# Normalising attention after the value product instead of before it

## The chip, the cores and the metric

The kernel runs on one core of one Trainium2 chip. The metric is device time in microseconds, from the first to the last instruction of one launch with what lies around it. The core has four compute engines with a queue each: TensorE (PE in the profile: matmuls and transposes, with its weight loads as PEld), VectorE (DVE), ScalarE (ACT) and GpSimd (POOL). A fifth queue, SyncE (SP), issues most of the transfers. The engines wait for each other by semaphores alone.

## The reference

One decoder block over x of 32 sequences of 32 tokens, width 512: cross attention to a context of 257 keys per sequence, then a retention layer, then a feed-forward layer with ternary weights. Only the cross attention is touched here:

```
Q, K, V = split_heads(q @ W_q + b_q), split_heads(k @ W_k + b_k), split_heads(v @ W_v + b_v)   # 16 heads of 32
scores = einsum('bhqd,bhkd->bhqk', Q, K) / sqrt(32); scores = where(mask == 0, -1e9, scores)
attn   = softmax(scores, axis=-1)
out    = einsum('bhqk,bhkd->bhqd', attn, V)          # then @ W_o + b_o, added to x
```

The value bias b_v is added after the value product (variable `bxv`), which is the same since each row of `attn` sums to one.

## The kernel before

The kernel has a start (queries of all 1024 tokens, until about 60 us), a loop over the 32 sequences (the cross attention, until about 510 us), and a tail over 8 tiles of 128 tokens (retention and feed-forward). The program of each engine is written out by hand in its own block, so each queue runs in the order of its code. The loop is software pipelined by one sequence: while the keys and values of sequence b are projected, the softmax and value product of b-1 are done. In the loop:

- **TensorE**, function `sequence` (L419): keys of b in four groups of 12 matmuls (all of them through the helper line L227; each float32 product is three products of float32r parts, high and low), the transpose `turn_mixed` of the result of b-2 (L417), the first half of the values (12 matmuls, L227), `turn` (L395: eight 128x128 transposes of the probabilities of b-1), the second half of the values, `mix` (L409, 64 small matmuls: probabilities times values of b-1), `score` (L386, 32 small matmuls: scores of b). L386 is the last of a sequence, and stands in the trace 32 times for each.
- **VectorE**, function `sequence` (L1086), for sequence b-1: four `mask_scores` (L1044, scaled and masked scores with the row minimum, from a PSUM bank to `probs`); `invert_sums` (L1051) and `normalise` (L1055) for two groups of heads and then for the other two; `keep_output` of b-2 (L1075); `split_context` for b+1 (L999 makes the high part of the context, L1001 the low part); `weigh_last` (L1063: the 257th key's probability times its value, since TensorE handles 256 keys); and `keep_mixed` (L1069: adds that to the value product out of PSUM, to `o_sb`).
- **ScalarE**: exponentials of `probs` with the row sum (L682), copies of keys (L677), values (L687) and of the turned probabilities (L692) out of PSUM. Exponentials 0 and 1 stand ahead of the copy of the first group of keys.
- **GpSimd**: copies the queries of a sequence (`pick_queries`, L870), which waits until the scores of an earlier one are done and so ties GpSimd to TensorE. Between these copies it quantises the feed-forward weights in eight chunks of 128x2048 float32 (`quantise_chunk`, L908, L910, L913: three steps, one chunk in two sequences), about from 190 to 405 us.

`turn` waits for the semaphore `probs_ready`, which L1055 raises; so the transposes stand behind the normalisation. `turn_mixed` waits for `mixed_kept`, which L1069 raises. TensorE starts the keys of b+1 only when `context_split` says that L1001 is done, and puts the fourth group of keys in the bank of the first, once ScalarE has kept that one.

Of the kernel before, what the change touches and what calls it, by code (L numbers as in the profile page):

```python
# [22 lines left out]
ALU = mybir.AluOpType  # L23
# [8 lines left out]
P = 128  # L32
B, S, D = 32, 32, 512
KEYS = 257
KPAD = KEYS + 1
H, DH = 16, 32
C = D // P
# [14 lines left out]
def build_block(nc, x, ctx_t, last_t, mask, ident, decay,  # L52
                w_xq, w_xk, w_xv, w_xo, w_q, w_k, w_v, w_g, w_o, w_1, w_2,
                b_xq, b_xk, b_xv, b_xo, b_g, b_o, gamma, beta, b_1, b_2, last_values, out):
    with ExitStack() as stack:
        def sb(name, shape, dt, offset):
            return nc.alloc_sbuf_tensor_at(name, [P] + shape, dt, offset=BASE + offset)
# [6 lines left out]
        def sem(name):  # L64
            return stack.enter_context(nc.semaphore(name))
# [10 lines left out]
        def vec(name, shape):  # L76

            nonlocal small_at
            t = sb(name, shape, F32, small_at)
            small_at += -(-4 * int(np.prod(shape)) // 32) * 32  # L80
            return t
# [9 lines left out]
        nmax, rowsum, rrow = vec("nmax", [C]), vec("rowsum", [C]), vec("rrow", [C])  # L91
# [31 lines left out]
        last_part, o_sb = sb("last_part", [C, DH], F32, at + 20 * K), sb("o_sb", [C, DH], F32, at + 20 * K + 512)  # L123
# [4 lines left out]
        probs = sb("probs", [C, KEYS], F32, at)  # L128
# [48 lines left out]
        keys_projected, keys_kept = sem("keys_projected"), sem("keys_kept")  # L177
        values_projected, values_kept = sem("values_projected"), sem("values_kept")
        scores_ready, scores_masked, exps_ready = sem("scores_ready"), sem("scores_masked"), sem("exps_ready")
        sums_inverted, probs_ready = sem("sums_inverted"), sem("probs_ready")  # L180
        probs_turned, probs_kept = sem("probs_turned"), sem("probs_kept")
        last_weighed, mixed, mixed_kept = sem("last_weighed"), sem("mixed"), sem("mixed_kept")
        mixed_turned, OT_kept = sem("mixed_turned"), sem("OT_kept")
# [27 lines left out]
        def later(n):  # L211

            return not isinstance(n, int) or n >= 1

        def hold(dve, place, signal, value):

            dve.wait_ge(signal, value)
            dve.memset(carrier[:, place:place + 1], 0.0)
# [101 lines left out]
        def _(pe):  # L320
# [68 lines left out]

            def turn(b):  # L390

                pe.wait_ge(probs_ready, 4 * b + 4)
                for half in range(2):
                    for g in range(C):
                        last = pe.transpose(bank[4 + half][:, g * P:(g + 1) * P],  # L395
                                            probs[:, g, half * P:(half + 1) * P], idf[:, :])
                    last.then_inc(probs_turned, 1)
# [21 lines left out]
            def sequence(b, par):  # L419

                project_keys(b, par)
                if later(b - 1):
                    turn_mixed(b - 2)
                project_values(b, par, 0)
                if later(b):
                    turn(b - 1)
                project_values(b, par, 1)
                score_inputs(b)
                if later(b):
                    mix(b - 1, 1 - par)  # L430
                score(b, par)
# [17 lines left out]
            project_output(0)  # L449
            project_output(1)  # L450
            turn(B - 1)
            project_output(2)
            mix(B - 1, 1)
# [388 lines left out]
        def _(pool):  # L842
# [6 lines left out]
            def invert_deviation(norm, eps, n, n_moments, moments, veps, rstd, t):  # L849

                _, mom, ve, rs = norm
                pool.wait_ge(moments, n_moments)
                pool.tensor_tensor(ve[:, 0:n], mom[:, 0:n, 1], eps[:, 0:n], ALU.add).then_inc(veps, 1)
                pool.wait_ge(veps, t + 1)
                pool.tensor_tensor(rs[:, 0:n], ve[:, 0:n], minus_half[:, 0:n], ALU.pow).then_inc(rstd, 1)
# [108 lines left out]
        def _(dve):  # L964
            def split_weight(n):
                dve.wait_ge(weights_high, n + 1)
                high, low = staged_weights[n][1]
                dve.tensor_tensor(low[:, :, :], stage[n % 2][:, :, :], high[:, :, :].bitcast(F32),
                                  ALU.subtract).then_inc(weights_low, 1)
# [24 lines left out]
            def split_context(b, par):  # L994
                dve.wait_ge(context_landed, 16 * b + 16)
                if later(b - 1):
                    dve.wait_ge(values_projected, 2 * (b - 1))
                high, low = ctxs[par]
                dve.tensor_copy(high[:, :, :], raw[:, :, :]).then_inc(context_high, 1)  # L999
                dve.wait_ge(context_high, b + 1)  # L1000
                dve.tensor_tensor(low[:, :, :], raw[:, :, :], high[:, :, :].bitcast(F32),  # L1001
                                  ALU.subtract).then_inc(context_split, 1)
# [36 lines left out]
            def mask_scores(b, g):  # L1039

                if g == 0 and later(b):
                    hold(dve, 5, last_weighed, b)
                hold(dve, g, scores_ready, 4 * b + g + 1)
                dve.tensor_tensor_reduce(out=probs[:, g, :], in0=bank[4 + g][:, 0:KEYS], in1=mbias[:, :], scale=-SCALE,  # L1044
                                         scalar=BIG, op0=ALU.add, op1=ALU.min,
                                         accum_out=nmax[:, g:g + 1]).then_inc(scores_masked, 1)

            def invert_sums(b, pair_):
                dve.wait_ge(exps_ready, 4 * b + 2 * pair_ + 2)
                part = slice(2 * pair_, 2 * pair_ + 2)  # L1050
                dve.reciprocal(rrow[:, part], rowsum[:, part]).then_inc(sums_inverted, 1)  # L1051

            def normalise(b, g):
                dve.wait_ge(sums_inverted, 2 * b + g // 2 + 1)
                dve.tensor_scalar(probs[:, g, :], probs[:, g, :], rrow[:, g:g + 1], None, ALU.mult).then_inc(probs_ready, 1)  # L1055

            def weigh_last(b, par, nth):

                dve.wait_ge(last_landed[par], 16 * nth + 16)
                if later(b):  # L1060
                    dve.wait_ge(mixed_kept, b)
                hold(dve, 6, probs_ready, 4 * b + 4)
                dve.tensor_tensor(last_part[:, :, :], v_last[par][:, :, :],  # L1063
                                  probs[:, :, KEYS - 1:KEYS].broadcast_to([P, C, DH]), ALU.mult).then_inc(last_weighed, 1)

            def keep_mixed(b):
                dve.wait_ge(last_weighed, b + 1)
                dve.wait_ge(mixed, b + 1)
                dve.tensor_tensor(o_sb[:, :, :], last_part[:, :, :], bank[3][:, 0:P].rearrange("p (g w) -> p g w", g=C),  # L1069
                                  ALU.add).then_inc(mixed_kept, 1)  # L1070

            def keep_output(b):

                dve.wait_ge(mixed_turned, b + 1)
                dve.tensor_tensor(OT[:, :, bass.ds(b * S, S)], bank[3][:, P:2 * P].rearrange("p (j q) -> p j q", j=HG),  # L1075
                                  bxv[:, :].unsqueeze(2).broadcast_to([P, HG, S]), ALU.add).then_inc(OT_kept, 1)

            def softmax(b):
                invert_sums(b, 0)
                normalise(b, 0)  # L1080
                normalise(b, 1)
                invert_sums(b, 1)
                normalise(b, 2)
                normalise(b, 3)

            def sequence(b, par, nth, more=True):  # L1086

                if later(b):
                    for g in range(C):
                        mask_scores(b - 1, g)  # L1090
                if later(b):
                    invert_sums(b - 1, 0)
                    normalise(b - 1, 0)
                    normalise(b - 1, 1)
                if later(b):
                    invert_sums(b - 1, 1)
                    normalise(b - 1, 2)
                    normalise(b - 1, 3)
                if later(b - 1):
                    keep_output(b - 2)  # L1100
                if more:
                    split_context(b + 1, 1 - par)
                else:
                    split_weight(3)
                if later(b):
                    weigh_last(b - 1, 1 - par, nth + par - 1)
                    keep_mixed(b - 1)
# [32 lines left out]
            def output_low(k):  # L1140
                dve.wait_ge(o_high, k + 1)
                part = slice(256 * k, 256 * k + 256)
                dve.tensor_tensor(oT[1][:, :, part], OT[:, :, part], oT[0][:, :, part].bitcast(F32),
                                  ALU.subtract).then_inc(o_low, 1)
# [14 lines left out]
                mask_scores(B - 1, g)  # L1159
            keep_output(B - 2)  # L1160
            output_low(1)
            softmax(B - 1)
            weigh_last(B - 1, 1, B // 2 - 1)
            output_low(2)
            add_output(0)
# [247 lines left out]
```

## Times and profile before

| what | value |
| --- | --- |
| median of 3 runs | 800.01 us (797.69 to 800.78) |
| the profiled execution | 796.09 us |
| its span | 794.1 us |
| TensorE busy | 744.9 us, 94% of the span |
| VectorE busy | 502.2 us, 63% |
| ScalarE busy | 328.4 us, 41% |
| GpSimd busy | 183.1 us, 23% |
| TensorE's mean granted clock | 0.991 |

The profiled execution spends 2.0 us outside its span. A busy time is a sum over the whole program; in the slices of the span one sees TensorE at nine tenths or more from the fourth slice to the last but few, and VectorE much busier in the stretch from about 180 to 410 us than before and after it, though its program is the same there. GpSimd is busy in just that stretch.

### The profile page before, as it was taken

The numbers are of one execution on the slowest core, as the hardware profiler recorded it, in microseconds if no ns is written. First come the engines' busy times: TensorE is split into PE (matmuls) and PEld (weight loads), VectorE is DVE, ScalarE is ACT, GpSimd is POOL, SyncE is SP. The second block draws the span as 40 slices with busy tenths as digits, with TensorE's granted clock in tenths as the row PEclk, the third lists the DMA queues.
The fourth block names the chain that finished last, engine by engine and source line by source line (L and its number), as shares of the span: only waits on it lengthen the run. The fifth ranks groups of instructions, "written<-read, shape, count | busy, mean of one in ns | idle before, by whom it ended". The sixth has DMA issues, their size and how long they took to land.

```text
span 794.1 us, 18836 instructions
## 1 busy us (share of the span) xinstructions
PE 744.9 (94%) x7449; PEld 609.4 (77%) x7464; DVE 502.2 (63%) x1228; ACT 328.4 (41%) x698; POOL 183.1 (23%) x150
## 2 busy tenths in 40 slices
PE   3999999999799999999999999999999999999985
PEld 2778888888687787787788888777777777777742
DVE  6334444345968778778664443485577877877785
ACT  2435464554343343343344444653233343342232
POOL 1500010005945455455420000001101111110010
PEclk9999999999999999999999999999999999999998
DMA  7142333330231231230120112541000000000000
GB/s 258 61 170 78 98 110 131 112 135 30 83 112 35 78 112 34 79 112 30 30 60 31 58 30 93 205 173 54 1 1 14 13 0 13 13 0 14 1 14 26
DMA packets 33956, 53.63 MB, mean 68 GB/s; under 512 B 2416, under 2 KB 23152, under 8 KB 32656
## 3 DMA queue, kind: packets, MB, share of 16 engines
q1 hardware_dynamic: 29168, 36.05, 13.9%
q0 software_dynamic: 3328, 16.78, 5.9%
q10 hardware_dynamic: 1440, 0.53, 0.3%
q8 instruction: 13, 0.21, 0.1%
q14 instruction: 7, 0.06, 0.0%
HBM read 51.19 MB, written 2.16 MB: 67 GB/s over the span
## 4 chain that ended last, share of the span: by engine, by line
PE 80%; issue 8%; DVE 7%; ACT 3%; DMA 1%; DVEq 0%; POOL 0%; SPq 0%; ACTq 0%; POOLq 0%
PE bank L227 56%; PE bank L566 4%; PE bank L395 3%; PE bank L550 3%; PE bank L409 3%; PE bank L515 3%; PE bank L503 2%; PE bank L386 2%; DVE probs L1055 2%; ACT probs L682 1%; DVE ctx_high L999 1%; PE bank L491 1%; PE bank L559 1%; DMA stage<-in_w_xo 1%; DMA X<-in_x 1%
## 5 line engine op out<-in xcount | busy, mean ns | idle before, releaser
L227 PE MATMUL bank<-ctx_high,wk_high 128*128 128x258 f32 x512 | 148.4, 290 | 3.9 <-DVE ctx_low L1001 3.7
L227 PE MATMUL bank<-ctx_low,wk_high 128*128 128x258 f32 x512 | 145.3, 284 | 0.0
L227 PE MATMUL bank<-ctx_high,wk_low 128*128 128x258 f32 x512 | 144.8, 283 | 0.0
L1055 DVE TENSOR_SCALAR probs<-probs,rrow 128x257 f32<-128x257 f32 x128 | 115.7, 946 | 2.3
L227 PEld LDWEIGHTS bank<-ctx_high,wk_high 128*128 128x128 f32 x512 | 97.4, 190 | 17.8 <-issue 17.1
L227 PE MATMUL bank<-wv_high,ctx_high 128*128 128x512 f32 x256 | 106.0, 414 | 0.0
L227 PE MATMUL bank<-wv_low,ctx_high 128*128 128x512 f32 x256 | 101.1, 395 | 0.0
L227 PE MATMUL bank<-wv_high,ctx_low 128*128 128x512 f32 x256 | 100.8, 394 | 0.0
L687 ACT ACTIVATE vals<-bank 128x512 f32<-128x512 f32 x64 | 38.2, 597 | 144.7 <-PE bank L227 144.7
L227 PEld LDWEIGHTS bank<-ctx_low,wk_high 128*128 128x128 f32 x512 | 97.5, 190 | 0.0
L227 PEld LDWEIGHTS bank<-ctx_high,wk_low 128*128 128x128 f32 x512 | 97.2, 190 | 0.0
L1069 DVE TENSOR_TENSOR o_sb<-last_part,bank 128x128 f32<-128x128 f32 x32 | 9.2, 287 | 121.9 <-PE bank L409 121.8
L677 ACT ACTIVATE kT<-bank,bxk 128x257 f32<-128x257 f32 x128 | 60.3, 473 | 59.2 <-PE bank L227 57.2
L682 ACT ACTIVATE probs<-probs,nmax 128x257 f32<-128x257 f32 x128 | 63.8, 501 | 35.1 <-DVE nmax L1044 35.1
L910 POOL TENSOR_SCALAR stage<-stage 128x2048 f32<-128x2048 f32 x8 | 57.1, 7138 | 0.7
L227 PEld LDWEIGHTS bank<-wv_high,ctx_low 128*128 128x128 f32 x256 | 48.1, 188 | 11.4
L1044 DVE CUSTOM_DVE_ANT_0 probs<-bank,mbias 128x257 f32<-128x257 f32 x128 | 47.5, 421 | 11.8 <-issue 11.8
L227 PEld LDWEIGHTS bank<-wv_high,ctx_high 128*128 128x128 f32 x256 | 48.2, 188 | 8.5
L227 PEld LDWEIGHTS bank<-wv_low,ctx_high 128*128 128x128 f32 x256 | 48.3, 188 | 8.4
L870 POOL COPY qs<-qT 128x128 f32<-128x128 f32 (+1 forms) x32 | 9.7, 304 | 184.2 <-PE bank L386 171.1
L395 PE MATMUL bank<-idf,probs 128*128 128x128 f32 x256 | 33.6, 274 | 12.9 <-DVE probs L1055 12.9
L395 PEld LDWEIGHTS bank<-idf,probs 128*128 128x128 f32 x256 | 29.3, 141 | 19.8 <-DVE probs L1055 16.4
(200 smaller groups left out, 1423.3 us busy)
## 6 DMA issues: line engine op xcount, KB each, us to landing
raw<-in_ctx_t SPq DMA_DIRECT2D x32, 514.0 KB, 3.9
stage<-in_w POOLq DMA_DIRECT2D x16, 1024.0 KB, 5.9
X<-in_x SPq DMA_DIRECT2D x4, 512.0 KB, 7.1
v_last<-last_values SPq DMA_DIRECT2D x32, 64.0 KB
out<-X SPq DMA_DIRECT2D x8, 256.0 KB, 2.0
stage<-in_w_xq SPq DMA_DIRECT2D x1, 1024.0 KB, 7.9
stage<-in_w_xk SPq DMA_DIRECT2D x1, 1024.0 KB, 13.1
stage<-in_w_xv SPq DMA_DIRECT2D x1, 1024.0 KB, 5.6
```

The lines of the kernel that those rows point to most:

```text
L227: last = pe.matmul(to, left(i, c), right(j, c), start=(c == 0 and i + j == 0), stop=(c == C - 1 and i == 1))
L395: last = pe.transpose(bank[4 + half][:, g * P:(g + 1) * P], probs[:, g, half * P:(half + 1) * P], idf[:, :])
L409: last = pe.matmul(bank[3][DH * j:DH * (j + 1), g * DH:(g + 1) * DH], pT[:, half, g, j * S:(j + 1) * S], vals[:, par, half, h * DH:(h + 1) ...
L515: last = pe.matmul(bank[7][DH * j:DH * (j + 1), g * P:(g + 1) * P], v_sb[:, h * DH:(h + 1) * DH], s_sb[:, j, g, :], start=True, stop=True)
L550: last = pe.matmul(bank[UP_BANK[n]][:, :], yqT[:, c, :], w1q[:, c, n * 512:(n + 1) * 512], start=(c == 0), stop=(c == C - 1))
L566: last = pe.matmul(bank[to][:, :], hqT[:, f, :], w2q[:, f, :], start=(f == 0), stop=(f == FC - 1))
L677: act.activation(kT[:, m, :], bank[m % 3][:, 0:KEYS], ACT.Identity, bias=bxk[:, m:m + 1]).then_inc(keys_kept, 1)
L682: act.activation(probs[:, g, :], probs[:, g, :], ACT.Exp, bias=nmax[:, g:g + 1], scale=-1.0, accum_out=rowsum[:, g:g + 1]).then_inc(exps_r ...
L687: act.activation(vals[:, par, half, :], bank[1 + half][:, :], ACT.Copy).then_inc(values_kept, 1)
L910: pool.tensor_scalar(at, at, ROUND, 1.0, ALU.subtract, ALU.min).then_inc(ffn_step, 1)
L1044: dve.tensor_tensor_reduce(out=probs[:, g, :], in0=bank[4 + g][:, 0:KEYS], in1=mbias[:, :], scale=-SCALE, scalar=BIG, op0=ALU.add, op1=ALU ...
L1055: dve.tensor_scalar(probs[:, g, :], probs[:, g, :], rrow[:, g:g + 1], None, ALU.mult).then_inc(probs_ready, 1)
```

## The change

The exponentials are no longer divided by their row sums before they are transposed and multiplied with the values. The four row-sum reciprocals become one instruction on 128x4, the four products on 128x257 go, and in `keep_mixed` one product on 128x128 is added: `o_sb` times the reciprocal, each of its four columns spread over the 32 columns of a head. The sum of L1069 then raises a new semaphore (`mixed_summed`), and the product raises `mixed_kept`. `turn` and `weigh_last` wait for the exponentials directly.

```
             def turn(b):
-                pe.wait_ge(probs_ready, 4 * b + 4)
+                pe.wait_ge(exps_ready, 4 * b + 4)
...
-            def invert_sums(b, pair_):
-                dve.wait_ge(exps_ready, 4 * b + 2 * pair_ + 2)
-                part = slice(2 * pair_, 2 * pair_ + 2)
-                dve.reciprocal(rrow[:, part], rowsum[:, part]).then_inc(sums_inverted, 1)
-
-            def normalise(b, g):
-                dve.wait_ge(sums_inverted, 2 * b + g // 2 + 1)
-                dve.tensor_scalar(probs[:, g, :], probs[:, g, :], rrow[:, g:g + 1], None, ALU.mult).then_inc(probs_ready, 1)
+            def invert_sums(b):
+                dve.wait_ge(exps_ready, 4 * b + 4)
+                dve.reciprocal(rrow[:, :], rowsum[:, :]).then_inc(sums_inverted, 1)
...
             def weigh_last(b, par, nth):
-                hold(dve, 6, probs_ready, 4 * b + 4)
+                hold(dve, 6, exps_ready, 4 * b + 4)
...
             def keep_mixed(b):
                 dve.wait_ge(last_weighed, b + 1)
                 dve.wait_ge(mixed, b + 1)
                 dve.tensor_tensor(o_sb[:, :, :], last_part[:, :, :], bank[3][:, 0:P].rearrange("p (g w) -> p g w", g=C),
-                                  ALU.add).then_inc(mixed_kept, 1)
+                                  ALU.add).then_inc(mixed_summed, 1)
+                dve.wait_ge(sums_inverted, b + 1)
+                dve.wait_ge(mixed_summed, b + 1)
+                dve.tensor_tensor(o_sb[:, :, :], o_sb[:, :, :], rrow[:, :].unsqueeze(2).broadcast_to([P, C, DH]),
+                                  ALU.mult).then_inc(mixed_kept, 1)
```

Only VectorE's queue changes its instructions. Its part of one sequence, from the last masked scores on, read before:

```order
L1051 RECIPROCAL rrow<-rowsum 128x2
L1055 TENSOR_SCALAR probs<-probs,rrow 128x257 x2
L1051 RECIPROCAL rrow<-rowsum 128x2
L1055 TENSOR_SCALAR probs<-probs,rrow 128x257 x2
L1075 TENSOR_TENSOR OT<-bank,bxv 128x4x32
L999 CAST ctx_high<-raw 128x1032
L1001 TENSOR_TENSOR ctx_low<-raw,ctx_high 128x1032
L218 MEMSET carrier 128x1
L1063 TENSOR_TENSOR last_part<-v_last_127,probs 128x128
L1069 TENSOR_TENSOR o_sb<-last_part,bank 128x128
```

And it reads now, with the lines of the changed file:

```order
L1050 RECIPROCAL rrow<-rowsum 128x4
L1074 TENSOR_TENSOR OT<-bank,bxv 128x4x32
L999 CAST ctx_high<-raw 128x1032
L1001 TENSOR_TENSOR ctx_low<-raw,ctx_high 128x1032
L218 MEMSET carrier 128x1
L1058 TENSOR_TENSOR last_part<-v_last_127,probs 128x128
L1064 TENSOR_TENSOR o_sb<-last_part,bank 128x128
L1068 TENSOR_TENSOR o_sb<-o_sb,rrow 128x128
```

Five instructions left the place between the masked scores and the sum out of PSUM (the row with x2 stands for two), and L1068 came in as the last one, directly ahead of the masked scores of the next sequence. The other place is VectorE's queue for the last sequence, where the output projection has begun. Before:

```order
L1075 TENSOR_TENSOR OT<-bank,bxv 128x4x32
L1143 TENSOR_TENSOR oT_low<-OT,oT_high 128x4x256
L1051 RECIPROCAL rrow<-rowsum 128x2
L1055 TENSOR_SCALAR probs<-probs,rrow 128x257 x2
L1051 RECIPROCAL rrow<-rowsum 128x2
L1055 TENSOR_SCALAR probs<-probs,rrow 128x257 x2
```

Now:

```order
L1074 TENSOR_TENSOR OT<-bank,bxv 128x4x32
L1128 TENSOR_TENSOR oT_low<-OT,oT_high 128x4x256
L1050 RECIPROCAL rrow<-rowsum 128x4
L218 MEMSET carrier 128x1
L1058 TENSOR_TENSOR last_part<-v_last_127,probs 128x128
L1128 TENSOR_TENSOR oT_low<-OT,oT_high 128x4x256
```

Here the last `turn` no longer stands behind the second `oT_low` (L1143 before, L1128 now) and the four products.

## Rows read from the trace of the kernel before

**Rows 1.** Waits of TensorE, 184 to 413 us: total, times, longest
```profile
PE bank L395 <- DVE probs L1055: 12.6, 7, 1.9
PE bank L227 <- DVE ctx_low L1001: 3.7, 1, 3.7
```
**Rows 2.** The chain of waits in time order: start, length, what
```profile
156.97 5.98 PE bank L227 x48
...
184.69 5.97 PE bank L227 x48
...
193.55 0.87 PE bank L395 x8
...
296.35 6.61 issue
...
303.81 1.09 PE bank L395 x8
...
309.04 5.97 PE bank L227 x48
```
**Rows 3.** Timeline of GpSimd: start, length, what
```profile
192.26 7.43 POOL L910 TENSOR_SCALAR stage<-stage 128x2048 f32<-128x2048 f32 x1
...
200.01 5.38 POOL L913 TENSOR_SCALAR w1q<-stage 128x2048 bf16<-128x2048 f32 x1
...
208.78 7.10 POOL L910 TENSOR_SCALAR stage<-stage 128x2048 f32<-128x2048 f32 x1
...
295.79 7.10 POOL L910 TENSOR_SCALAR stage<-stage 128x2048 f32<-128x2048 f32 x1
309.40 0.29 POOL L870 COPY qs<-qT 128x128 f32<-128x128 f32 x1 [6.52 <-PE bank L386]
309.66 5.37 POOL L913 TENSOR_SCALAR w2q<-stage 128x2048 bf16<-128x2048 f32 x1
```
**Rows 4.** Timeline of VectorE while GpSimd quantises
```profile
192.76 5.43 DVE L1001 TENSOR_TENSOR ctx_low<-raw,ctx_high 128x1032 fp32r<-128x1032 f32 x1
198.12 0.28 DVE L1063 TENSOR_TENSOR last_part<-v_last,probs 128x128 f32<-128x128 f32 x1
...
208.97 7.47 DVE L999 CAST ctx_high<-raw 128x1032 fp32r<-128x1032 f32 x1
...
294.94 8.10 DVE L1055 TENSOR_SCALAR probs<-probs,rrow 128x257 f32<-128x257 f32 x2
```
**Rows 5.** Durations of two lines, ns: minimum, median, maximum
```profile
L1055 DVE TENSOR_SCALAR probs<-probs,rrow x128: 333/354/7265, 61.9 to 517.2; 128x257 f32<-128x257 f32 x128
L1063 DVE TENSOR_TENSOR last_part<-v_last,probs x32: 280/287/3717, 65.8 to 517.8; 128x128 f32<-128x128 f32 x32
```
**Rows 6.** Windows, L386 alone: stretch, length, TensorE busy (count), PEld, clock, DMA
```profile
115.43:143.14 27.71, 1.43 (x64) 0.47 (x64) 1.00 0.37 118
184.69:412.36 227.67, 10.74 (x480) 3.48 (x480) 0.99 0.21 67
184.69:233.60 48.91, 2.15 (x96) 0.70 (x96) 0.97 0.23 79
233.60:398.45 164.85, 7.87 (x352) 2.55 (x352) 1.00 0.20 62
```
**Rows 7.** Windows, all work: PE, PEld, DVE, ACT, POOL busy, clock, DMA
```profile
217.84:221.84 4.00, 4.00 (x20) 4.00 (x21) 3.83 (x3) 0.00 (x0) 4.00 (x1) 0.57 0.00 0
```
**Rows 8.** Timeline of VectorE in an undisturbed sequence
```profile
163.47 0.70 DVE L999 CAST ctx_high<-raw 128x1032 fp32r<-128x1032 f32 x1
164.20 1.23 DVE L1001 TENSOR_TENSOR ctx_low<-raw,ctx_high 128x1032 fp32r<-128x1032 f32 x1
...
170.31 0.29 DVE L1069 TENSOR_TENSOR o_sb<-last_part,bank 128x128 f32<-128x128 f32 x1 [4.66 <-PE bank L409]
```
**Rows 9.** Timeline of ScalarE: the first copy of keys of the sequence from 184.69
```profile
186.38 0.48 ACT L677 ACTIVATE kT<-bank,bxk 128x257 f32<-128x257 f32 x1
```
**Rows 10.** Timeline of TensorE: the last sequence's transposes
```profile
517.64 1.09 PE L395 MATMUL bank<-idf,probs 128*128 128x128 f32 x8 [0.32 <-DVE probs L1055]
```

More of the change, by code:

```diff
@@ L179, in build_block @@
         scores_ready, scores_masked, exps_ready = sem("scores_ready"), sem("scores_masked"), sem("exps_ready")
-        sums_inverted, probs_ready = sem("sums_inverted"), sem("probs_ready")
+        sums_inverted, mixed_summed = sem("sums_inverted"), sem("mixed_summed")
         probs_turned, probs_kept = sem("probs_turned"), sem("probs_kept")
@@ L1076, in keep_output @@
                                   bxv[:, :].unsqueeze(2).broadcast_to([P, HG, S]), ALU.add).then_inc(OT_kept, 1)
[L1078 to L1084, printed above, removed]
             def sequence(b, par, nth, more=True):
@@ L1091, in sequence @@
                 if later(b):
[L1092 to L1098, printed above, removed]
+                    invert_sums(b - 1)
                 if later(b - 1):
@@ L1161, in _ @@
             output_low(1)
-            softmax(B - 1)
+            invert_sums(B - 1)
             weigh_last(B - 1, 1, B // 2 - 1)
```

## The prediction, made before the changed kernel ran

> **What bounds the kernel now.** I read the busy times first. The reader sees TensorE at work for nearly the whole span and VectorE for under two thirds, so time taken off VectorE is worth nothing where TensorE doesn't wait for it. The waits of TensorE tell where it does: between 184 and 413 us it waits seven times for L1055, 12.6 us, and once for L1001, 3.7 us [rows 1]. The chain of waits shows such a place: 6.6 us in which VectorE has a product in hand and waits for nothing that the profile names, and behind them the transposes of TensorE [rows 2]. GpSimd's timeline beside it gives the cause. L910 runs there from 295.79 to 302.89 [rows 3], and the two normalisations that began at 294.94 take 8.10 us, until 303.0 [rows 4]; the line takes 0.354 us in the median and 7.265 at most [rows 5]. This product can't run beside GpSimd's quantisation and stands until that is done.
>
> How much this costs: an undisturbed pair of sequences takes 27.71 us with 64 score matmuls, 32 for each sequence [rows 6], so one sequence takes 13.855. From 184.69 to 412.36 us there are 480 / 32 = 15 sequences in 227.67 us [rows 6]; undisturbed they take 207.83. The quantisation costs 19.8 us. By windows [rows 6]: the 3 sequences up to 233.60 take 48.91 instead of 41.57 (7.3 lost); the next 11 take 164.85 instead of 152.41 (12.4 lost, in six waits, one for each pair); what is left is 0.05. Of the 7.3, 3.7 is the wait for L1001 and some 1.5 the seventh wait for L1055 [rows 1]. In the 4.00 us after the longer one the granted clock is 0.57, between its levels of 1.2 and 2.4 GHz [rows 7], where it is 1.00 in an undisturbed stretch [rows 6]: 4.00 x 0.43 = 1.7 us.
>
> **The change part by part.** *Removed: four products and one reciprocal in each sequence.* Undisturbed they are about 1.4 us of VectorE (4 x 0.354, [rows 5]), worth nothing, since the pair of 27.71 has them. In the disturbed stretch they carry the wait. `turn` comes 193.55 - 184.69 = 8.86 us after the start of a sequence [rows 2]. Two exponentials are done before the first copy of keys at 1.7 (186.38, [rows 9]) and two follow it, so all four are ready before 4, and neither ScalarE nor L1044 (out of PSUM) is held by GpSimd. The six waits go.
>
> *What is late next.* The block doesn't vanish: the next instruction that GpSimd can hold is the cast L999, which took 7.47 us once [rows 4] and takes 0.70 alone [rows 8]. It asks at 163.47 - 156.97 = 6.5 us after a sequence's start [rows 2, 8]. Take the sequence with the L910 at 295.79. It ends at 309.04 [rows 2] and takes 13.86 + 12.4 / 6 = 15.9, so it begins at 293.1. The cast would ask at 299.6, get through at 302.9 with the end of L910 and end at 303.6; L1001 takes 1.23 more [rows 8] and ends at 304.8. TensorE wants it for the next keys at 293.1 + 13.86 = 306.95: 2.1 us are to spare. L1069 waits for the value product until 170.31 - 156.97 = 13.3 anyway [rows 2, 8]. In the other sequence of a pair L913 runs from 0.62 to 6.0 after the start (309.66 for 5.37, start 309.04, [rows 2, 3]) and is over before the cast asks. GpSimd's copy L870 waits for scores [rows 3], so this phase holds in all six pairs. The gain is 12.4, and 0.05 with the last sequence.
>
> *The start of the stretch.* Here GpSimd's steps are not tied to scores. Before, L1055 stood until the L913 from 200.01 was done, and so the cast came behind the second L910 and took until 216.4 [rows 3, 4], L1001 until 217.7. Now the cast of that sequence (start 184.69 + 13.86 = 198.55) asks at 205.0, waits for that L913's end at 205.4, and is done by 206.1, L1001 by 207.4; TensorE wants it at 212.4. The 3.7, the 1.5 and the slow clock go: 7.3. One sequence on, the cast asks at 218.9, the next L913 ends between 221.7 and 222.7 (the second, if VectorE holds GpSimd up by a microsecond at 206), and L1001 is done by 224.6, wanted at 226.3: 1.7 to spare.
>
> *Added: one product on 128x128, L1068.* The nearest row is L1063, the same size with both inputs in SBUF: 0.287 us in the median, 3.717 at most [rows 5]. It stands ahead of the next masked scores, so these, the exponentials and ScalarE's first copy of keys behind two of them move by some 0.3. TensorE needs that copy for its fourth key group, three quarters of 5.97 = 4.5 us after the start [rows 2]; it is done at 186.86 - 184.69 = 2.2 [rows 9]. That leaves 2.3. In the six pairs L1068 runs from 13.65, when GpSimd is still waiting for scores (its copy starts 309.40 - 309.04 = 0.36 after the next start, [rows 2, 3]): free. Only near 212.2 would it meet an L910, the one that starts at 208.78 before [rows 3] and at 208.8 to 209.8 now. L1001 met the L910 of 192.26 and took 5.43, 4.2 longer than alone [rows 4, 8]; but L910's recorded end is 199.69, and L1001 ended at 198.2 and L1063 ran in 0.28 at 198.12 [rows 3, 4]. So a product with two inputs is let through before GpSimd's recorded end, about 4.7 us after L910's start (192.76 + 4.2). L1068 would come through at 213.5 to 214.5, the scores 1.2 to 2.2 us late, inside the 2.3. If it stood until the recorded end (216 to 217), the copy of keys would end near 219, wanted at 216.9: 2 us of TensorE. I take 0, by the row of the same size, with bounds of 0 and 2. Below nothing it can't go, since it takes no work away.
>
> The Trainium skill, "SBUF — State Buffer", section "Who interferes with whom", says that a VectorE instruction with two SBUF inputs contends with a GpSimd instruction that reads SBUF, and that the loser blocks fully, for the whole instruction of the other. By its letter L1068 stands until L910's end, and the sum would be 2 us less. The row of L1063 at 198.12 speaks for an earlier release.
>
> *The last sequence.* `turn` waits 0.32 us for the last product [rows 10], which goes: 0.3. There L1068 falls behind the value product while 12 output matmuls run ahead of the transpose that wants it: 0.
>
> Sum: 12.4 + 0.05 + 7.3 + 0.3 - 0 = 20.1 us. The profiled execution took 796.09 us, 2.0 outside its span of 794.1; it would take 776.0, with a span of 774. The median of the runs shown is 3.9 higher, 800.01, and the same gain gives 779.9, rounded to 780.
>
> **The rivals.** *The start keeps part of its loss.* For: its slacks are small, 1.7 and 0.1 to 1.1, and a wait there costs clock as well [rows 7]. Against: 5 us of slack at the place where it waited before. Price up to 7.3: 787.
>
> *The cast takes the product's place.* For: it is held in every pair, for 3.3 us. Against: 2.1 of slack. Were TensorE to wait for it as it did for L1055, the 12.4 would stay: 792.
>
> *The product was not what `turn` waited for*; the profile names only who came last. Then nothing moves: 800. Against: the end of L910 and the transposes stand together in the rows [rows 2, 3].
>
> *The other side: L1068 is held in every pair.* It has two SBUF inputs and stands ahead of all that a sequence makes of its scores. Were GpSimd to read across the end of a sequence, L1068 would be held 3.4 us (3.717 - 0.287, [rows 5]) to 7.1 (L910, [rows 3]); beyond 2.3 of slack that is 1.1 to 4.8 for each of 15 sequences, 17 to 72 us against 20 gained: 797 to 852. It decides from the point where L870 no longer waits for scores. In the row it waits 6.52 us [rows 3].
>
> **How the numbers follow.** Forecast 0.76; part of the start stays 0.11; cast late 0.05; nothing 0.04; L1068 held 0.04. Half a per cent, 4 us, is about what can be told from no change here. The first three are faster, 0.92; the fourth and the mild end of the fifth are the same, 0.05; slower 0.03. The low end is the forecast for the profiled execution, 776.0, and half a microsecond of scatter: 775.5. The high end takes in the first rival: 787.5.
>
> **What would show it.** Right: TensorE has no wait for VectorE between 184 and 413 us, pairs take 27.7 there as elsewhere, some six or seven casts take 4 us, at most one or two of the two-input products are long, and the clock is 1.00 after 217 us. Wrong: waits of L227 for L1001 in each pair (the cast), of L227 for ScalarE's copy of keys (L1068), or pairs of 29.8 still.

## The result, and the profile after

| | before | after |
| --- | --- | --- |
| median | 799.55 us (4 runs) | 775.5 us (4 runs, 773.9 to 776.97) |
| ratio | 1 | 0.9701 (95%: 0.9668 to 0.9734) |
| in five further rounds | 798.35 us | 776.9 us, 0.9719 (0.9694 to 0.9744) |
| span of the profiled execution | 794.1 us | 772.1 us |
| TensorE's mean granted clock | 0.991 | 0.993 |

The changed kernel is 21 to 24 us faster. I had forecast 780.0, a gain of 20, and a range of 775.5 to 787.5: the time lies on the very edge of the range. The kernel before was profiled in an execution of 796.09 us, the changed one in one of 773.9. One run of the kernel before, beside the five further rounds, took 2244.52 us at a granted clock of 0.33, and no ratio has it in.

In the lines below, L1050 is the reciprocal, L1058 the old L1063, L1064 the old L1069, and L1068 the new product. The waits of TensorE in the last sequence (the answer to [rows 1]; between 183 and 392 us the same view lists none at all):

```profile
PE bank L227 <- DVE oT_low L1128: 1.2, 1, 1.2
...
PE bank L417 <- DVE o_sb L1068: 0.2, 1, 0.2
```

Windows, with the score matmuls alone, as in [rows 6] (stretch, length, TensorE busy and count, PEld, clock, DMA):

```profile
72.42:183.39 110.97, 5.73 (x256) 1.86 (x256) 1.00 0.36 119
183.39:391.65 208.26, 10.74 (x480) 3.49 (x480) 1.00 0.23 73
238.93:377.76 138.83, 7.16 (x320) 2.33 (x320) 1.00 0.23 73
```

The 15 sequences beside GpSimd's quantisation take 208.26 us where they took 227.67: 19.41 us less, and 0.43 more than 15 undisturbed ones. Five pairs take 138.83, so one takes 27.77. The clock, which was 0.57 for 4 us in this stretch [rows 7], is 1.00.

The timeline of VectorE shows where the block went. First at the start of the quantisation, then in a regular pair:

```profile
203.69 0.77 DVE L999 CAST ctx_high<-raw 128x1032 fp32r<-128x1032 f32 x1
204.49 1.23 DVE L1001 TENSOR_TENSOR ctx_low<-raw,ctx_high 128x1032 fp32r<-128x1032 f32 x1
205.65 2.32 DVE L1058 TENSOR_TENSOR last_part<-v_last,probs 128x128 f32<-128x128 f32 x1
...
210.98 1.60 DVE L1068 TENSOR_TENSOR o_sb<-o_sb,rrow 128x128 f32<-128x128 f32 x1
...
217.65 3.60 DVE L999 CAST ctx_high<-raw 128x1032 fp32r<-128x1032 f32 x1
...
259.19 3.88 DVE L999 CAST ctx_high<-raw 128x1032 fp32r<-128x1032 f32 x1
263.11 1.23 DVE L1001 TENSOR_TENSOR ctx_low<-raw,ctx_high 128x1032 fp32r<-128x1032 f32 x1
```

And GpSimd beside it:

```profile
207.92 7.10 POOL L910 TENSOR_SCALAR stage<-stage 128x2048 f32<-128x2048 f32 x1
...
255.43 7.10 POOL L910 TENSOR_SCALAR stage<-stage 128x2048 f32<-128x2048 f32 x1
...
267.02 0.29 POOL L870 COPY qs<-qT 128x128 f32<-128x128 f32 x1 [4.50 <-PE bank L386]
```

These lines show three things. The cast L999 takes 3.88 us in the pair and ends at 263.07, half a microsecond after L910's end at 262.53; L1001 is done at 264.34, while the next keys start at 266.66: 2.3 us to spare. Seven casts take 3.6 us or more, this one and the one at 217.65 among them. L1068 was held only once, at 210.98; it takes 0.29 us in the median. And GpSimd still waits 4.50 us for the scores, which keeps L910 away from L1068.

**Where the 22.0 us between the two spans lie**, from the starts of the same matmuls in both chains of waits and the windows:

| stretch (before; after) | before | after | less |
| --- | --- | --- | --- |
| until the third sequence (73.81; 72.42) | 73.81 | 72.42 | 1.39 |
| 8 undisturbed sequences | 110.88 | 110.97 | -0.09 |
| 15 beside the quantisation | 227.67 | 208.26 | 19.41 |
| 6 undisturbed | 83.14 | 83.17 | -0.03 |
| the last sequence and the output | 29.76 | 28.91 | 0.85 |
| the tail's steady part | 216.65 | 216.65 | 0 |
| the end | 52.19 | 51.72 | 0.47 |

The first 1.39 is no work of the change: the programs are the same there. The chain after the first wait of TensorE, before:

```profile
17.71 5.46 PE bank L227 x12
```

and after:

```profile
17.70 4.42 PE bank L227 x12
```

The same 12 matmuls take 5.46 or 4.42 us, and the 8 transposes behind them 1.25 or 0.87; in both traces the matmuls begin at 0.63 us each and fall to 0.39, after 22.54 in the trace before and after 20.40 in the one after. This 1 us and more is chance: in the second profile of the changed kernel the 12 take 5.03, with the long steps cut (e4) 5.46, and in a kernel with the old softmax (e9) 4.55. It looks like the clock, but the records don't show that: the granted clock from 17 to 23.16 us stands at 1.00 in these profiles. The 0.47 at the end lies where the two windows show clocks of 1.00 and 0.86 before, 0.89 and 0.90 after.

### The profile page after: what moved, and what is told of

Its sections match the earlier page's. It is cut to its first block, busy times and chain, and to the rows that moved or that the text cites. A ratio compares the mean times of both kernels' runs of the same rounds, so it can differ in the third digit from the quotient of the medians.

```text
span 772.1 us, 18699 instructions
## 1 busy us (share of the span) xinstructions
PE 741.4 (96%) x7464; PEld 608.0 (79%) x7464; DVE 408.4 (53%) x1100; ACT 325.5 (42%) x698; POOL 184.0 (24%) x150
## 4 chain that ended last, share of the span: by engine, by line
PE 94%; DVE 4%; ACT 1%; issue 1%; DMA 1%; POOL 0%; DVEq 0%; POOLq 0%
PE bank L227 68%; PE bank L550 4%; PE bank L395 4%; PE bank L566 4%; PE bank L409 3%; PE bank L515 3%; PE bank L386 3%; PE bank L503 2%; PE bank L491 1%; PE bank L559 1%; DMA X<-in_x 1%; PE bank L465 1%; PE bank L522 0%; DVE h_max L1221 0%; PE bank L354 0%
## 5 line engine op out<-in xcount | busy, mean ns | idle before, releaser
L1064 DVE TENSOR_TENSOR o_sb<-last_part,bank 128x128 f32<-128x128 f32 x32 | 9.2, 288 | 123.0 <-PE bank L409 123.0
L910 POOL TENSOR_SCALAR stage<-stage 128x2048 f32<-128x2048 f32 x8 | 57.1, 7138 | 0.7
L1074 DVE TENSOR_TENSOR OT<-bank,bxv 128x128 f32 (+1 forms) x32 | 9.3, 292 | 78.1 <-PE bank L417 78.0
L999 DVE CAST ctx_high<-raw 128x1032 fp32r<-128x1032 f32 x32 | 45.1, 1410 | 1.9 <-DMA raw<-in_ctx_t 1.9
L1001 DVE TENSOR_TENSOR ctx_low<-raw,ctx_high 128x1032 fp32r<-128x1032 f32 x32 | 43.7, 1365 | 1.1
```

What stands on the lines that cost most here:

```text
L910: pool.tensor_scalar(at, at, ROUND, 1.0, ALU.subtract, ALU.min).then_inc(ffn_step, 1)
```

## The experiments

Each ran beside the kernel before on the same chip; times are medians, ratios with 95% intervals.

**The product in another form.** The kernel before, with an added row sum that nobody reads:

```
-                dve.tensor_scalar(probs[:, g, :], probs[:, g, :], rrow[:, g:g + 1], None, ALU.mult).then_inc(probs_ready, 1)
+                dve.tensor_scalar(probs[:, g, :], probs[:, g, :], rrow[:, g:g + 1], 0.0, ALU.mult, ALU.add,
+                                  accum_out=spare_sum[:, g:g + 1]).then_inc(probs_ready, 1)
```

> The kernel before with its four products kept, in their old place and with turn still waiting for them, but each also writes the sum of its row to a spare column. Theory A (the product is held by GpSimd because it takes the second port of SBUF that the two engines share): in this form it takes one port, is never held, costs 0.35 to 0.45 us each time, and TensorE has no wait for L1055 or L1001 between 184 and 413 us. About 19 us of the loop come back as in the changed kernel; only the wait of the last sequence stays: 776 to 779 us. Rival B (VectorE has too much work ahead of the transposes, whatever its form): the work is the same or a little more, so 799 to 801 us. Rival C (any instruction of VectorE that reads and writes SBUF is held): products of 7 us stay, 799 to 801 us.

777.74 us, ratio 0.9733 (0.9693 to 0.9772). The products (minimum, median, maximum in ns) and the cast in its trace:

```profile
L1056 DVE TENSOR_SCALAR_CACHE_REDUCE probs<-probs,rrow x128: 474/480/484, 61.1 to 497.4; 128x257 f32<-128x257 f32 x128
...
L1000 DVE CAST ctx_high<-raw x32: 686/700/3954, 42.9 to 467.9; 128x1032 fp32r<-128x1032 f32 x32
```

A slower product (0.48 instead of 0.354, [rows 5]) that is never held gives back all but 1 to 2 us of what the change gave, with the whole softmax in its old place and more work on VectorE. The cast takes the block, as in the changed kernel. Rivals B and C fall. This is a rule of the Trainium skill too ("SBUF — State Buffer", "Who interferes with whom": the form that also writes out its accumulator stays out of the two-port modes), and the trace agrees, 0.484 at most against 7.265.

**The products back in their place, but not in front of the transposes.** The changed kernel with, in `invert_sums`,

```
+                dve.wait_ge(sums_inverted, b + 1)
+                for g in range(C):
+                    if later(b) or g >= 2:
+                        dve.wait_ge(spared, 4 * b + g - 1)
+                    dve.tensor_scalar(spare[g % 2][:, :], probs[:, g, :], rrow[:, g:g + 1], None, ALU.mult).then_inc(spared, 1)
```

> The changed kernel with four products of the old form in the old place, whose results go to a spare tile that nobody reads, so turn does not wait for them. They are held by GpSimd as before. If the gate in front of the transposes was the cost (theory A): the six waits of a pair go (12.4 us) with the seventh (1.5) and the last (0.3), but at the start of the quantisation the cast again falls behind the second long step of GpSimd, and the wait of 3.7 us for L1001 with the slow clock behind it (1.7) stays: 783 to 787 us. If the work on VectorE is the cost (rival B): all stays, 798 to 801 us. If neither the held product nor its place matter any more once turn is free: 775 to 777 us.

778.7 us, ratio 0.9754 (0.9713 to 0.9794): 3.2 us over the changed kernel's 775.5, 4 us and more under what I expected. Its only new wait in the loop, among TensorE's waits:

```profile
PE bank L229 <- DVE ctx_low L1003: 2.6, 1, 2.6
```

So the direction is right: with the gate gone, the six pairs lose nothing by held products (the products, L1057 here, have a mean of 0.79 us, and a pair takes 27.70), and what stays is the wait for the context at the start, where the pair from 183.94 to 214.48 took 30.54. I had put that wait at 3.7 with 1.7 of clock, as before. Here the cast stood 2.63 us and the instruction behind it, L1003, 5.42, together less than the 8.7 before [rows 4, 8]; the wait was 2.6, and the granted clock in the 4 us after it 1.00.

**GpSimd's steps cut.** Both kernels with `at, to = at[:, 0:16], to[:, 0:16]` ahead of L908, and the rest of the quantised weights set to zero.

> The kernel before with GpSimd's three quantising steps done on 16 of 2048 columns of a chunk (the rest of the quantised weights is zero), so that GpSimd holds nothing for long. Theory A: every sequence takes 13.86 us, products stay at 0.35 us, and 19.8 us go: 776 to 780 us. Rival B: VectorE's work is what it was, 799 to 801 us.

> The changed kernel with the same cut of GpSimd's steps. Theory A: there is nothing left for GpSimd to cost, since its holds of the cast are hidden: 774 to 776.5 us, within 1 us of the changed kernel and 0.3 to 1 us under e3. If holds still cost the changed kernel something: up to 3 us less than 775.5.

Before with the cut: 776.94 us, 0.9723 (0.9683 to 0.9763). After with the cut: 775.55 us, 0.9709 (0.967 to 0.9749). Without GpSimd's long steps the kernel before is 23 us faster, and the changed one no faster than these runs can tell (775.55 and 775.5). The two cut kernels differ by 1.4, with intervals that overlap: without GpSimd's long steps the change by itself is worth that much at most, and perhaps nothing.

**The rival on the other side, made on purpose.** The changed kernel, in which a chunk waits longer before L908:

```
                 pick_queries(2 * n - 6, 0, half)
+                pool.wait_ge(probs_turned, 2 * (2 * n - 8) + 2)
                 quantise_chunk(n, lambda: pick_queries(2 * n - 5, 1, half))
```

> The changed kernel, in which each quantised chunk of GpSimd waits until the transposes of a sequence are done, 9.9 us after the sequence's start, so that its long step L910 lies over the end of the sequence, where L1068 stands. This is the mechanism of the rival on the other side, made on purpose, in six pairs. Theory A (a product with two inputs in SBUF is let through some 4.7 us after L910's start, before its recorded end): L910 runs from 12.0 after the start, L1068 is done at 17.0, the masked scores start 3.1 us late, the first copy of keys ends at 5.2 after the next start and TensorE wants it at 4.5: 0.7 to 1 us for each pair, 4 to 6 in all, 779 to 782 us, with a wait of TensorE for ScalarE's copy of keys. Rule B (held until L910's end at 19.1): 5.2 us late, 3 us for each pair, 18 in all and some slow clock: 793 to 800 us. C (L1068 isn't held by GpSimd): 775 to 776 us.

The second waits for `values_projected, 2 * (2 * n - 7) + 1` instead:

> The same with the chunk waiting for the first half of the values, 8.9 us after the start, so that L910 runs from 11.0 to 18.1. Theory A: L1068 is held from 13.7 until 16.0, the masked scores start 2.1 us late, the first copy of keys ends at 4.2 and is wanted at 4.5: 775 to 777 us, though L1068 takes 2.3 us or more in six pairs. Rule B (held until 18.1): 2 us for each pair, 12 in all: 787 to 790 us. C: as A in time, but L1068 at 0.29 us everywhere.

The third for `probs_kept, 2 * (2 * n - 8) + 2`:

> The changed kernel with each quantised chunk of GpSimd waiting until ScalarE has kept the turned probabilities, 10.5 us after a sequence's start. In the trace of e5 the long step L910 started 11.85 after the start, L1068 was done 4.66 after that, and pairs of sequences took 28.05 instead of 27.75: the slack was just used up. Here L910 starts at 12.55 and L1068 is done at 17.2, 0.7 later. Theory A (release 4.66 after L910's start; each tenth beyond the slack is a tenth of TensorE): pairs of 28.6 to 28.8, six of them, 5 to 6 us above the changed kernel: 780 to 783 us, with TensorE waiting for ScalarE's first copy of keys in the chain. Rule B (release at L910's end): 2.4 more for each pair, above 793 us. C (the pairs of e5 had another cause): 776 to 778 us.

| | L1068 at most | a pair takes | median | ratio |
| --- | --- | --- | --- | --- |
| e6, wait until 8.9 us | 1.99 us | 27.92 us | 777.52 us | 0.9732 (0.9706 to 0.9758) |
| e5, until 9.9 us | 2.86 us | 28.05 us | 778.33 us | 0.9744 (0.972 to 0.9767) |
| e7, until 10.5 us | 3.60 us | 28.79 us | 783.56 us | 0.9794 (0.9766 to 0.9823) |

The changed kernel took 776.9 beside e5 and e6. Only e7 came out about as expected, half a microsecond above its range: L1068 was held in seven pairs, not six. e5 stayed under its 779 to 782, and its trace has no wait of TensorE for the copy of keys. In e6 the time is half a microsecond over its range and L1068 under the 2.3 us I had put down. In e7 the waits of TensorE, 180 to 510 us, and VectorE's and GpSimd's timelines at one pair:

```profile
PE bank L227 <- ACT kT L677: 5.8, 8, 0.8
```

```profile
240.87 3.58 DVE L1069 TENSOR_TENSOR o_sb<-o_sb,rrow 128x128 f32<-128x128 f32 x1
```

```profile
239.79 7.10 POOL L910 TENSOR_SCALAR stage<-stage 128x2048 f32<-128x2048 f32 x1
```

The product (L1069 in these kernels) is done at 244.45, 4.66 us after L910 began and 2.4 before its recorded end at 246.89. It was 4.66 in e5 as well (L910 at 237.91, done at 242.57), in e6 (236.81, done at 241.47) and in the changed kernel itself (207.92, done at 212.58). So rule B, held until the end, is refuted in four kernels. In e7 the first copy of keys is the next thing late, as the prediction's rival on the other side said, and pairs of sequences take 28.79 us (from 227.16 to 255.95). In e5, with L910 starting 11.85 us after a sequence's start, the chain that ended last already runs through the held product and the copy of keys: the slack is just used up. In e6 a pair takes 0.15 longer than in the changed kernel; its copies of keys are in time, and the trace names no wait for this.

**Only GpSimd moved, the softmax left alone.** The kernel before, with the wait of e5:

> The kernel before, softmax and all, with GpSimd's chunks only moved: each waits until the transposes of a sequence are done, 9.9 us after its start. Theory A (the gain was the place of the block, not the work): L910 runs from 11.9 to 19.0, so the products, which come 2.9 us after the next start, stand until 5.1 and are done before 7, and turn wants them at 8.86; the six waits go, 12.4 us. The start of the stretch is not moved and keeps its 7.3. About 786 to 789 us. Rival B (normalising ahead of the transposes costs by itself): 797 to 801 us.

797.25 us, 0.9972 (0.9955 to 0.9989): a miss by 8 to 11 us. The timelines of VectorE and of GpSimd, in this kernel:

```profile
276.11 3.81 DVE L1056 TENSOR_SCALAR probs<-probs,rrow 128x257 f32<-128x257 f32 x2
...
280.02 5.52 DVE L1056 TENSOR_SCALAR probs<-probs,rrow 128x257 f32<-128x257 f32 x2
```

```profile
272.31 7.10 POOL L910 TENSOR_SCALAR stage<-stage 128x2048 f32<-128x2048 f32 x1
...
279.73 5.41 POOL L913 TENSOR_SCALAR w1q<-stage 128x2048 bf16<-128x2048 f32 x1
```

I had looked at L910 alone. L913 begins at 279.73, 0.3 us after L910's end, and holds the second pair of products, which stands until 285.5; `turn` still waits, 17.2 us in seven times. By itself this run looks like rival B. So the next one moved both steps, L908 and L910 behind the transposes of one sequence, L913 behind those of the next:

```
-                quantise_chunk(n, lambda: pick_queries(2 * n - 5, 1, half))
+
+                def between():
+                    pick_queries(2 * n - 5, 1, half)
+                    pool.wait_ge(probs_turned, 2 * (2 * n - 7) + 2)
+                pool.wait_ge(probs_turned, 2 * (2 * n - 8) + 2)
+                quantise_chunk(n, between)
```

> The kernel before, softmax and all, with both parts of GpSimd's chunks moved: L908 and L910 wait until the transposes of one sequence are done, L913 until those of the next are. In e8 only the first was moved; there L910 held the first pair of products until 5.1 us after the start, and L913 followed at once and held the second pair until 10.7, so turn still waited 2.45 us, seven times. Theory A (the gain of the change is the place of the block): now only L910 meets the products and lets them go at 5.1, L913 runs where no product stands, turn comes at 8.86 without a wait, also at the start of the stretch: 19 us of the loop come back without any change to the softmax, 778 to 782 us. Rival B (normalising ahead of the transposes costs by itself, and e8 showed that): 795 us or more. Between (the start keeps its part): 784 to 788 us.

777.98 us, 0.9738 (0.9708 to 0.9768). The window of the 15 sequences, and VectorE's products (L1060 here) in one of them:

```profile
183.45:391.58 208.13, 10.73 (x480) 3.48 (x480) 1.00 0.23 73
```

```profile
268.57 3.83 DVE L1060 TENSOR_SCALAR probs<-probs,rrow 128x257 f32<-128x257 f32 x2
272.50 0.62 DVE L1060 TENSOR_SCALAR probs<-probs,rrow 128x257 f32<-128x257 f32 x2
```

Here 19.5 us come back, as with the change, with the normalisation in place and 3.8 us of held products in each pair. Two waits on GpSimd do what the new softmax does.

**The changed kernel again.**

> The changed kernel as it is, in more rounds, to get the gain with a narrower interval and to see how far the granted clock of the first matmuls moves it from run to run. By the traces 20.3 us of the gain belong to the change (19.4 in the loop and 0.85 in the last sequence) and 1.9 to the clock at the start and at the end of the profiled runs: a gain of 20 to 22 us over the kernel before if the clock is chance, 24 if it is not.

776.9 us against 798.35, a gain of 21.5: within what was expected if the clock is chance. The five times run from 774.48 to 777.81, and go with the mean clock: 0.993 for the fastest, 0.989 for the two slowest. But chance alone it is not: the mean clock was 0.989 to 0.993 in the nine runs of the changed kernel, and 0.981 to 0.989 in the 34 others of the kernel before that stood beside the experiments. Its profiled execution, at 0.991 and 796.09 us, was quicker than every one of these. In e8, the other kernel whose transposes wait in each pair, the trace shows where some of the clock goes: it is 0.57 from 223 to 227 us, after TensorE had waited 2.54 us for products, and 0.62 from 316 to 320, after 2.42 us. The profile of the kernel before has one such place and 1.00 from 300 to 320 us; the changed kernel has 1.00 in both. So a wait can cost clock behind it, and the gain between medians may well hold more of this than the profiled pair shows. That is argued, not shown: how large that part is stays open, since no execution of the kernel before near its median was profiled.

## Why the prediction was right, and where its sizes were off

- **The cause.** That products of 257 columns stand behind GpSimd's steps and `turn` behind them: shown three ways, by taking the hold off the product (e1), by taking the long steps away (e3) and by moving them (e9).
- **Six pairs, 12.4 us.** Sized right: a pair takes 27.77 us. Without GpSimd's long steps (e4) it takes 27.71, so the 0.05 or so above that belongs to them; by which way was not looked into.
- **The cast is late next, and hidden.** Held as forecast, to within 0.2 us of L910's end; 2.3 us were to spare where I said 2.1.
- **The start, 7.3 us.** The whole stretch gave 19.41 of the 19.84 forecast (12.4, 7.3 and what was rounded off), so this term lost 0.4 at most. The cast that I saw held until 205.4 hardly was (0.77 us); the one behind it was, as forecast (3.60), with 2.5 us to spare.
- **L1068 free, 0 with a bound of 2.** It was held once, and done 4.66 us after L910's start; I had it let through at 4.7 and so done at 5.0. TensorE waited for nothing in that stretch. The bound by the full hold didn't happen, and e7 shows what a hold beyond the slack costs. The sign that at most one or two of the two-input products are long was too strict: L1001 took 5.43 once, L1058 2.32 and L1068 1.60.
- **The last sequence, 0.3 us.** This term was too small: 0.85. From the starts of the same matmuls, 0.51 of it lies between the first output matmul and the transposes (6.04 us before, 5.53 after), where the profile gives a wait of 0.32, and 0.25 ahead of the fourth group of keys, where a wait of 0.2 for a copy of keys went. The idle time of the profile is counted from a modelled end of the matmul before, and it is too small a price for a wait: in the pairs, too, a wait of at most 1.9 us [rows 1] cost 12.4 / 6 = 2.07. The two output rows above changed nothing: the wait for `oT_low` fell from 1.5 to 1.2, and a new one of 0.2 for L1068 stands just ahead of it, where I had none.
- **The step from the span to the time.** The sum was made against an execution of 796.09 and then set on the median of 800.01. The span came out at 772.1 where I had 774, and 1.9 of the 22.0 between the spans lie at the start and the end, where the programs are the same. The gain, not the level, was what the trace could give: 20.3 us lie where the change is (19.41 and 0.85), against the 20.1 of the sum. The medians moved by more, 21.5 and 24, and the clock of the kernel before was lower in all its other runs with a clock on record than in the profiled one; the sum left that out. The scatter of 2 to 3 us from run to run should have widened the low side of the range. That 775.5 still lies in it is luck.
- **The rival on the other side** was priced for each of 15 sequences, but L910 runs in every second one. In e7 seven products were held, and the loss was 1 us for each.
- **The chance of 0.76** for the forecast's mechanism can't be judged by one result. What I would have got wrong is e8's lesson: a block that moves off one step of GpSimd can fall under the next.

## What to carry to other kernels

When an engine's product has a median of 0.35 us and a maximum of 7, look at which instruction of the neighbouring engine ends with it before asking how much work can be removed. The remedy is to take the held instruction off the path, to write it in a form that isn't held, or to move the neighbour's long steps to where nothing stands: all three gave 21 to 24 us here, and in the traces the 15 sequences beside the quantisation take 208.26, 208.27 (e1) and 208.13 us (e9) instead of 227.67. The last two leave the mathematics alone. Before moving such a step, list every instruction that it could hold and every step that follows it at once.

## What the runs showed of the hardware

- A VectorE product of 128x128 with two SBUF inputs beside GpSimd's L910 (128x2048 float32, 7.10 us) is done 4.66 us after L910's start, in four kernels, 2.4 us before its recorded end. A cast or a product of float32 with one input stands until about the recorded end: the cast L999 from 259.19 to 263.07, 0.54 after L910's end and 0.70 long by itself; in e8 two products from 276.11 to 279.92, with L910's end at 279.41. The Trainium skill, "SBUF — State Buffer", "Who interferes with whom", has the loser blocked for the whole instruction; for the two-input form beside L910 the measurement differs. It doesn't beside the shorter step L908: L1058 stood from 205.65 to 207.97 in the changed kernel, and L908 ran from 205.87 to 207.83.
- The product with an accumulator takes 0.48 us, and 0.084 for reading the sum out, against 0.354 without one: the form that can be held is the faster one as long as GpSimd is quiet.
